# A transformer's attention scores in two passes: the second pass on 64 rows of the array, two column pieces beside one another

## The reference, cut to what matters

```python
q = ((x @ Wq[l].T + bq[l]) * scaling).reshape(n, H, DH)      # n = 1250, H = 8, DH = 64
k = (x @ Wk[l].T).reshape(n, H, DH)
v = (x @ Wv[l].T).reshape(n, H, DH)
scores = jnp.einsum('ehd,ehd->eh', q[tgt], k[srcidx])
# softmax of the scores over the edges of each target, then
agg = jax.ops.segment_sum(w[:, :, None] * v[srcidx], tgt, num_segments=n)
```

## Time and profile before

| | |
|---|---|
| timed runs | median 1790.54 us (1788.01 to 1790.7, 3 runs) |
| profiled execution | 1782.27 us |
| its span, first to last instruction | 1780.4 us |
| mean granted TensorE clock | 0.955 |
| PE busy | 1635.2 us (92%) |
| PE weight loads busy | 1511.8 us (85%) |
| DVE busy | 1307.7 us (73%) |
| ACT busy | 1164.9 us (65%) |
| score matmuls L1926 | 142.4 + 89.6 us, 576 + 384 of them |
| transposes L1936 | 191.4 us, 1600 of them |
| weighing matmuls L1947 | 189.5 us, 3200 of them |

### The profile page before, as it was taken

How to read it: one execution, slowest core, us unless ns; L and a number is a source line. 1 busy time by engine, 2 the same in 40 slices (tenths; PEclk the granted TensorE clock), 3 DMA queues, 4 the chain that set the end, 5 groups by cost and what they waited for, 6 DMA issues and landing times. The chain is left out here.

```text
span 1780.4 us, 34835 instructions
## 1 busy us (share of the span) xinstructions
PE 1635.2 (92%) x14082; PEld 1511.8 (85%) x14082; DVE 1307.7 (73%) x2329; ACT 1164.9 (65%) x2102; POOL 37.3 (2%) x53
## 2 busy tenths in 40 slices
PE   6898999999979999998979999998797999999971
PEld 3786999999859999998968888888796888888871
DVE  6995999997568999877247778756722777777577
ACT  3454788898648888776447788772433778887323
POOL 0000000000000000000000000002000000000020
PEclk9999899999989999899989999999898999999995
DMA  5113223200025221104964234003077133200204
GB/s 178 53 57 99 71 74 103 83 30 1 1 60 168 88 88 59 59 1 119 259 152 119 59 79 96 2 11 120 1 181 199 63 76 71 66 2 1 60 0 122
DMA packets 73355, 139.33 MB, mean 78 GB/s; under 512 B 16269, under 2 KB 44773, under 8 KB 71912
## 3 DMA queue, kind: packets, MB, share of 16 engines
q1 hardware_dynamic: 73192, 137.06, 27.4%
HBM read 96.22 MB, written 29.45 MB: 71 GB/s over the span
## 5 line engine op out<-in xcount | busy, mean ns | idle before, releaser
L1017 PE MATMUL banks<-h,probs_t_gat 125*125 125x128 f32 (+1 forms) x3200 | 376.2, 274 | 0.0
L1017 PEld LDWEIGHTS banks<-h,probs_t_gat 125*125 125x125 f32 x3200 | 367.2, 191 | 0.0
L2022 DVE CUSTOM_DVE_ANT_0 probs_att<-banks,logs_or_y 125x1250 f32<-125x1250 f32 x160 | 233.6, 1460 | 147.8 <-PE banks L1926 146.6
L1982 ACT COPY probs_t_att<-banks 125x375 f32<-125x375 f32 (+1 forms) x480 | 205.4, 533 | 76.3 <-PE banks L1936 76.2
L1974 ACT ACTIVATE probs_att<-probs_att,neg_max_att 125x1250 f32<-125x1250 f32 x160 | 218.4, 1365 | 49.6 <-DVE neg_max_att L2022 49.6
L1003 PE MATMUL banks<-ident,probs_gat 125*125 125x125 f32 x1600 | 214.7, 283 | 20.6 <-ACT probs_gat L1091 20.6
L1235 DVE CUSTOM_DVE_ANT_0 probs_gat<-probs_gat,log_counts 125x1250 f32<-125x1250 f32 x160 | 232.7, 1455 | 0.1
L1091 ACT ACTIVATE probs_gat<-probs_gat,neg_max_gat 125x1250 f32<-125x1250 f32 x160 | 212.8, 1330 | 20.5 <-DVE neg_max_gat L1235 20.0
L1003 PEld LDWEIGHTS banks<-ident,probs_gat 125*125 125x125 f32 x1600 | 195.3, 196 | 24.4 <-ACT probs_gat L1091 24.3
L1936 PE MATMUL banks<-ident,probs_att 125*125 125x125 f32 x1600 | 191.4, 275 | 0.0
L1100 ACT COPY probs_t_gat<-banks 125x1250 f32<-125x1250 f32 x160 | 190.0, 1188 | 2.1 <-PE banks L1003 2.1
(11 more groups left out here) (231 smaller groups left out, 2548.2 us busy)
## 6 DMA issues: line engine op xcount, KB each, us to landing
a_pair<-a_src_rows SPq DMA_DIRECT2D x46, 625.0 KB, 4.8
q_first<-q_rows SPq DMA_DIRECT2D x12, 1000.0 KB, 10.8
logs_or_y<-log_rows SPq DMA_DIRECT2D x20, 546.9 KB
q_rows<-q_out_qkv SPq DMA_DIRECT2D x40, 250.0 KB, 4.5
q_att<-q_rows SPq DMA_DIRECT2D x8, 1000.0 KB, 10.6
w_rows<-in_L_gnn_W_dram SPq DMA_DIRECT2D x12, 512.0 KB, 14.5
log_counts<-counts_fr SPq DMA_DIRECT2D x50, 122.1 KB
k_halves<-k_low_qkv SPq DMA_DIRECT2D x20, 250.0 KB, 4.2
```

The costliest lines, as they stand in the source:

```text
L1017: total = pe.matmul(out_bank(u), probs_t[:, u % KEPT, i], rows, start=i == 0, stop=i == T - 1)
L1982: act.copy(probs_t[:, u % TURNED, lo:hi].rearrange("p c n -> p (c n)"), turned(u, j)).then_inc(piece_saved, 1)
L2022: dve.tensor_tensor_reduce(probs[:, u % SLOTS], scores, logs[:, t % KEPT], -1.0, -FLOOR, ALU.add, ALU.min, neg_max[:, column(u)]).then_inc ...
```

## The change

The first pass stays. The second pass multiplies q's low part with k's high part only, on the 64 partitions that hold it (`own`). From unit 4 on its middle piece (columns 512 to 1023) takes q's low part and k's high part from the other 64 partitions: a new tile `k_beside` holds those columns of k's high part there, filled by two DMAs at the start of the attention stage. The product of q's low part and k's low part is no longer computed. To make room, two tiles of logs stay on chip instead of four (`KEPT`), and `k_beside` lies where the third and fourth were.

```diff
+        self.k_beside = gat.ROWS + gat.HALF // 2
...
             store_k(3)
             store_q(3)
-            load_logs(2)
-            load_logs(3)
             store_k(4)
             store_q(4)
             sp.wait_ge(x_stored, 16)
-            sp.wait_ge(prefetched, 160)
+            sp.wait_ge(prefetched, 96)
...
-    KEPT = 4
+    KEPT = 2
+    BESIDE = 4
...
+        k_beside = at("k_beside", [2 * CH, H // 2, BANK], F32R, places.k_beside)
+        beside = k.sem(f"beside_att{k.layer}")
...
+            for odd in range(2):
+                sp.dma_start(k_beside[(1 - odd) * CH:(2 - odd) * CH].bitcast(F32),
+                             k_halves[odd * CH:(odd + 1) * CH].rearrange("p (c odd) n -> p odd c n", odd=2)[:, odd, :, BANK:2 * BANK]
+                             .bitcast(F32)).then_inc(beside, 16)
             for r in range(T // 2):
...
-                for t in (2 * r + 2, 2 * r + 3):
-                    if KEPT <= t < T:
+                for t in (2 * r, 2 * r + 1):
+                    if t >= KEPT:
                         load_logs(t)
                     if biased:
-                        load_x(t - 2)
+                        load_x(t)
...
-                for half in range(2):
-                    for a, width in pieces(N):
-                        total = pe.matmul(scores[:, a:a + width], q[r % 2][:, h, half, t % 2 * P:(t % 2 + 1) * P],
-                                          k_halves[:, h, a:a + width], start=half == 0, stop=half == 1)
+                if u == BESIDE:
+                    pe.wait_ge(beside, 32)
+                dst = slice(t % 2 * P, (t % 2 + 1) * P)
+                own, other = (slice(i * CH, (i + 1) * CH) for i in (h % 2, 1 - h % 2))
+                for a, width in pieces(N):
+                    pe.matmul(scores[:, a:a + width], q[r % 2][:, h, 0, dst], k_halves[:, h, a:a + width], start=True, stop=False)
+                for a, width in pieces(N):
+                    if a == BANK and u >= BESIDE:
+                        total = pe.matmul(scores[:, a:a + width], q[r % 2][other, h, 1, dst], k_beside[other, h // 2],
+                                          start=False, stop=True)
+                    else:
+                        total = pe.matmul(scores[:, a:a + width], q[r % 2][own, h, 1, dst], k_halves[own, h, a:a + width],
+                                          start=False, stop=True)
```

## The result

| | before | after |
|---|---|---|
| timed runs, median | 1786.8 us | 1794.9 us |
| ratio of after to before | | 1.0058, 95% interval 1.0045 to 1.0072 |
| profiled span | 1780.4 us | 1791.5 us |

The changed kernel is slower by 0.6%, some 10 us; the spans differ by 11.1 us. The medians are only 8.1 us apart, since the runs of either kernel lie in groups a few us apart by their mean granted clock (0.948 to 0.957), so that a median moves with the mix, and one run of the kernel before (1943.45 us) isn't in the ratio. (The median of before is from 20 runs side by side with the changed kernel; the one shown above the prediction is from three of them.)

A forecast was written before the change was run, and what follows sets the result against it. The prediction took PE to bound the attention stage. Its terms, +9.1 us for the pairs and +1.6 for units 0 to 3, gave +10.7 on 1790.5, so 1801 us, range 1784 to 1814.

The forecast's parts named there:

- the case that was forecast: Second pass on PE: halves overlap, but added changes of shape cost more; 1801 us, within 1797 to 1806, chance 0.60.
- PE bounds, the rest is free: Attention stage: PE busy throughout, DVE and ACT with time to spare; copy and mask tiles taken as 0.
- A change of shape keeps the next load back 0.196 and lays 0.104 of load bare: PE, between kinds of matmul: first load 0.196 us after the last matmul's start, then 0.104 us bare.
- The two halves overlap fully: Second pass from unit 4 on: the matmul on the other half hides all of a 512-column matmul, 0.231 us.
- Per pair +0.12: Second pass, units 4 to 79: 0.03 us less before weighing, 0.15 more before transposes; 76 pairs, +9.1 us.
- The start +1.6: Units 0 to 3, both layers: 64-row pass without a partner lengthens each score by 0.19 us, +1.6 us in all.
- free changes: Rival: changes between full array and 64 rows cost nothing; 0.46 us less per pair, 1755 us, chance 0.13.
- missing overlap: Rival: the other half's matmul starts only when the first is done; +35 us, 1836 us, chance 0.10.
- unit 4 and the mask tiles: Rival of a late load, k_beside at unit 4 or a mask tile: 1801 plus 4 to 10 us, chance 0.06.
- the rival with a cheaper way out: Some switches cheaper, such as 64 rows to full with its load hidden: -15 us, 1786 to 1796, chance 0.11.

The follow-up runs named there:

- the even units: Changed kernel with the 64-row second pass only in even units from unit 4 on, all others on 128 rows: ratio 0.9992 to the kernel before, pair 6.93 us.
- the odd ones: Changed kernel with the 64-row second pass only in odd units from 5 on, all others on 128 rows: pair 7.11 us, start 25.50 / 24.32.
- the change that was taken away: Changed kernel, but odd units from 5 on do the 64-row pass before the full pass: ratio 0.9986 to the kernel before, pair 6.89 us.
- the start with its four units alone: Changed kernel with the 64-row second pass only in units 0 to 3, later units on 128 rows: first score to first weighing 24.52 / 24.94 us.
- the kernel without a partner: Changed kernel with the second pass's middle piece run after the first on the unit's own 64 rows: ratio 1.0261 to the kernel before, pair 7.53 us.

## Why the prediction was right

The forecast of the time was 1801 us, and 1794.9 was measured: inside the stated range (1784 to 1814), but below the 1797 to 1806 of the case that was forecast. Some 4 us of the difference are the starting point: three runs had put the kernel before at 1790.5, twenty put it at 1786.8. The change itself was forecast as +10.7; the ratio stands for about +10, the spans differ by 11.1.

- **PE bounds, the rest is free.** Shown: PE busy through the whole stretch in both kernels; with the PE part undone, the rest of the change makes no difference.
- **A change of shape keeps the next load back 0.196 and lays 0.104 of load bare, for 64 rows too.** Shown at both borders: 0.19 from the last matmul to the load. This was the step taken from rows at 1 and 40 partitions. The Trainium skill, "TensorEngine Tiling (Array Packing)", Key Properties, says that a change of tiling mode drains the engine; the trace agrees: the load doesn't start with the preceding matmul there, and each added change costs 0.18 to 0.19 us, the same by the even units (0.23 saved, 0.04 left), by the odd ones (two changes, 0.23 saved, 0.13 lost in all) and by the change that was taken away (0.18). The Trainium skill, "TensorE: Matmul & The Clock Gate", Measured speedup vs the span model, has a pack take one matmul and about 4 ns for each further tile; the trace agrees for the pack itself (starts 0.01 apart or less). That rule has no term for a pack that must be entered and left: a pair would be 6.5 us by it, against 7.06 measured.
- **The two halves overlap fully.** Shown: 0.46 us per pair, against 0.46 taken.
- **Per pair +0.12.** Measured +0.09: before weighing a gain of 0.04 (0.03 was taken; the same sum without rounding gives 0.037), before transposes a loss of 0.13 (0.15 taken). The terms are small differences of larger ones, taken from rows rounded to 0.01. From the first to the last weighing matmul that is 3.5 us per layer, 7.0 in all, instead of 9.1.
- **The start +1.6.** This term was mis-sized: +2.5 and +2.3 us, 4.8 in all. One cause is the price itself. At the half clock of the start a way in takes 0.27 to 0.28 us (units 0 and 1: 4.27 and 4.30 us from score to score against 3.99 and 4.03), not the 0.19 that was read at full clock; and behind unit 2 the way out doesn't fall into a wait, since transposes follow (2.67 us against 2.26). The other cause is the granted clock, which the sum held the same. In layer 0 the transposes behind unit 5 ran at 0.56 and took 1.7 us more. In layer 1 the score of unit 3 still ran at the lower clock for most of its time (2.24 us against 1.25), while the slow stretch around unit 5 was there before as well, at another place: score and transposes together 5.12 us against 4.95. That the start with its four units alone came out 0.8 and 0.7 longer, close to the 0.8 taken, is in part chance, in layer 1 by the balance told above. What decides when the clock falls isn't settled.
- The sum of the two, 7.0 + 4.8 = 11.8, less 0.7 outside the attention stages, is the 11.1 of the spans; that 10.7 was forecast comes in part from two errors with opposite signs. This was luck.

The rivals: free changes would have given a pair of 6.5, missing overlap 7.5 (that is what the kernel without a partner shows), and unit 4 and the mask tiles wait for no DMA. The measured 1794.9 us lies among the 1786 to 1796 of the rival with a cheaper way out, but its mechanism isn't there: the way from 64 rows to transposes keeps the load back 0.19 us and lays it bare, as the way in does.

## What to carry to other kernels

Packing two matmuls on halves of the array does give the full overlap, but count the changes of the array's shape around it: each added one costs 0.18 to 0.19 us, nearly as much as the 0.23 us that a hidden 512-column matmul saves. Put the packed work at borders where the shape changes anyway (here on both sides of weighing): with the same matmuls that took a pair from 7.06 us to 6.88, against 6.97 before. And leave the 64-row pass out where it has no partner and stands on the critical chain, as in units 0 to 3 here, where it saves nothing and each way in lengthens the chain. Both together turned +0.6% into -0.4% in the profiled attention stages (ratio 0.9943 by the timed runs). Last, look for changes of the granted clock in both layers of the kernel before too: a slow stretch that seems to come with an edit may have been there already.

## What the runs showed of the hardware

- Weight loads for the two halves of the rows start together, too (1061.38 twice), so one load time of 0.10 us is bare per change, not two.
- The wait at a change of shape is about the same in and out, for columns and for rows: at full clock 0.19 to 0.20 us from the start of a last matmul of about 0.1 us to the next load, between scores, transposes and weighing alike.
- At a granted clock of 0.50 an added way into 64 rows lengthened the time from score to score by 0.27 to 0.28 us.
- The granted clock can fall to half behind the same wait of PE on DVE (1.56 us ahead of unit 5's score) in one kernel and stay up in another, and in one layer of a kernel and not in the other (0.73 against 1.00 in the kernel before). No run here shows what decides it.
